# Second attention: the order of a batch's eight projection jobs, with the value job of the batch's own tokens moved from place 5 to place 7

## What is computed

```python
q = (draft_hidden @ Wq.T).reshape(bsz, draft_len, H, HD)          # H = 16 heads, HD = 128
kv_in = jnp.concatenate([context_hidden, draft_hidden], axis=1)   # 128 context + 128 own tokens
k = (kv_in @ Wk.T).reshape(bsz, total_len, KVH, HD)               # KVH = 4
v = (kv_in @ Wv.T).reshape(bsz, total_len, KVH, HD).transpose(0, 2, 1, 3)
q = _rope(_rms_norm(q, q_norm_w), draft_position_ids)
k = _rope(_rms_norm(k, k_norm_w), full_position_ids)
probs = jax.nn.softmax(jnp.einsum('bhqd,bhkd->bhqk', q, k) * SCALE, axis=-1)
attn = jnp.einsum('bhqk,bhkd->bhqd', probs, v)
return attn @ Wo.T
```

## Time and profile before

| what | value |
|---|---|
| median of 3 runs | 3103.31 us (3097.90 to 3106.26) |
| profiled execution | 3106.21 us, span 3104.41 us, mean granted TensorE clock 0.97 |
| busy in the span: PE, DVE, ACT, POOL | 2848.2, 1829.6, 1703.5, 1741.2 us |
| second attention | about 2026 to 2814 us of the span |
| its steady part, 2116 to 2760 us: PE, DVE, ACT, POOL busy | 600.91, 555.51, 441.20, 417.19 of 644 us |

### The profile page before, as it was taken

How to read it: one execution, slowest core, us unless ns; L and a number is a source line. 1 busy time by engine, 2 the same in 40 slices (tenths; PEclk the granted TensorE clock), 3 DMA queues, 4 the chain that set the end, 5 groups by cost and what they waited for, 6 DMA issues and landing times. The chain is left out here.

```text
span 3104.4 us, 57661 instructions
## 1 busy us (share of the span) xinstructions
PE 2848.2 (92%) x16353; PEld 1637.9 (53%) x16354; DVE 1829.6 (59%) x5590; ACT 1703.5 (55%) x4562; POOL 1741.2 (56%) x2443
## 2 busy tenths in 40 slices
PE   4699999999999969999999999769999999985998
PEld 2366666666666635555555554335444444443665
DVE  4366666666666655444344344458888888863443
ACT  5578777877778732333233223346666666661332
POOL 6467777777777534554444455366666666631222
PEclk9799999999999989999999999889999999997999
DMA  6711121112111153554555456535555545657444
GB/s 241 251 42 56 51 86 48 48 55 79 58 48 55 54 200 120 161 157 125 147 159 151 137 141 186 141 80 113 122 113 123 122 112 122 123 106 286 80 83 70
DMA packets 467529, 360.89 MB, mean 116 GB/s; under 512 B 295520, under 2 KB 366304, under 8 KB 467424
## 3 DMA queue, kind: packets, MB, share of 16 engines
q1 hardware_dynamic: 404912, 282.85, 32.1%
q0 software_dynamic: 16496, 37.79, 6.3%
q10 hardware_dynamic: 46016, 38.99, 4.4%
HBM read 186.23 MB, written 110.39 MB: 96 GB/s over the span
## 5 line engine op out<-in xcount | busy, mean ns | idle before, releaser
L1393 POOL TENSOR_TENSOR e_st<-e_st,e_ws_tile 128x1024 f32<-128x1024 f32 x64 | 123.8, 1935 | 428.1 <-PE e_y L1149 417.2
L752 ACT ACTIVATE a_nrm<-a_mm,a_sc_t 128x128 f32<-128x128 f32 x768 | 290.8, 474 | 123.6 <-POOL a_sc_t L905 123.4
L603 DVE BATCH_NORM_STATS2 a_st<-a_mm 128x6 f32<-128x128 f32 x768 | 170.7, 285 | 289.5 <-PE a_mm L440 206.5
L439 PE MATMUL a_mm<-a_w_hi,a_xq_hi 128*128 128x512 f16 x768 | 296.6, 386 | 22.7 <-POOL a_xq_lo L887 15.7
L1187 ACT ACTIVATE e_hh<-e_ha 128x512 f16<-128x512 f32 x128 | 76.3, 596 | 411.7 <-PE e_ha L1134 410.1
L440 PE MATMUL a_mm<-a_w_hi,a_xq_lo 128*128 128x512 f16 x768 | 296.4, 386 | 0.0
L1282 DVE SCALAR_TENSOR_TENSOR e_hl<-e_ha,e_hh 128x512 f16<-128x512 f32 x128 | 88.4, 691 | 351.6 <-ACT e_hh L1187 351.2
L904 POOL TENSOR_TENSOR a_sc_t<-a_sc_t,a_mhalf 128x4 f32<-128x4 f32 x192 | 203.2, 1058 | 119.0 <-DVE a_sc_t L610 118.7
L1147 PE MATMUL e_y<-e_w2h,e_hh 128*128 128x512 f16 x640 | 242.6, 379 | 0.0
L1148 PE MATMUL e_y<-e_w2l,e_hh 128*128 128x512 f16 x640 | 242.6, 379 | 0.0
L1149 PE MATMUL e_y<-e_w2h,e_hl 128*128 128x512 f16 x640 | 242.6, 379 | 0.0
(11 more groups left out here) (366 smaller groups left out, 8246.6 us busy)
## 6 DMA issues: line engine op xcount, KB each, us to landing
e_st<-in_w SPq DMA_DIRECT2D x128, 512.0 KB, 4.2
disp<-a_empty SPq DMA_DIRECT2D x16, 2084.0 KB
e_st<-in_w1b SPq DMA_DIRECT2D x32, 352.0 KB, 3.1
disp<-a_empty SPq DMA_DIRECT2D x4, 2605.0 KB, 22.8
e_xb<-disp SPq DMA_DIRECT2D x40, 260.5 KB, 4.3
e_xb<-disp ACTq DMA_DIRECT2D x40, 260.5 KB
a_cx<-in_ctxT SPq DMA_DIRECT2D x32, 256.0 KB, 3.3
a_stage<-in_wprojT SPq DMA_DIRECT2D x16, 512.0 KB, 4.7
```

The source lines that it names most:

```text
L439: pe.matmul(out, xq_hi[:, n, c, :], w_hi[:, t, c, :], start=(c == 0), stop=False)
L752: ins = act.activation(nrm[:, n % 2, i * P:(i + 1) * P], src[:, i * P:(i + 1) * P], ACT.Identity, bias=sc_t[:, n % 2, 3, i:i + 1], scale=s ...
```

## The change

In the list of jobs, VD moves from place 5 to place 7; Q2 and Q3 move one place forward, to 5 and 6. `NORM1`, `V1`, the waits on banks and all buffers by even and odd follow from the list. No instruction is added or left out.

```diff
-JOBS1 = ["KC", "KD", "Q0", "VC", "Q1", "VD", "Q2", "Q3"]
+JOBS1 = ["KC", "KD", "Q0", "VC", "Q1", "Q2", "Q3", "VD"]
 NJ1 = len(JOBS1)
 NORM1 = [t for t, j in enumerate(JOBS1) if j[0] != "V"]
 V1 = [t for t, j in enumerate(JOBS1) if j[0] == "V"]
```

## The result

The changed kernel takes 3117.18 us (median of 4 runs, 3112.62 to 3119.38) against 3102.64 us (3097.9 to 3106.26) for the kernel before, run beside it: ratio 1.0046, 95% interval 1.0034 to 1.0058. It is slower by about 14.5 us, more than the 0.3% (9.3 us) that the prediction took as the least that can be told from no change. The profiled execution took 3116.52 us (span 3114.7).

The account below looks back on a forecast made before the run. The prediction took a closed ring of engines waiting for each other as the bound, TensorE only following. 14 periods gave +14.0 us, the first batch +1, the last -2: +13 on the 3103.31 median, 3116 us, range 3099 to 3134.

Parts of the forecast that it names:

- the ring: VectorE, GpSimd, ScalarE and SyncE wait for each other from slot 5 to the next slot 5, 46.02 us a batch.
- the ends: First and last batch, outside the 14 periods: +1 us for the first, -2 us for the last.
- GpSimd's queue: Slots 5 and 6: job 5's scales, tables, then job 6's scales put job 6's normalisation 3.0 us later, disturbance included.
- The collisions: GpSimd operations lengthened beside VectorE: +0.4 us on the tables, 0.5 us on job 6's five short operations.
- rival 1: No collision on GpSimd: a period changes by about 0, 3102 us; chance 0.26.
- rival 3: Full exclusion between VectorE and GpSimd: both collisions at their upper end, 1.4 us more a period, 3136 us; chance 0.15.
- Slot 7 to slot 1: VectorE: value's low half adds 0.60 us, job 7's 1.47 us wait goes; slot 1's low probabilities start 1.4 us later.
- TensorE: Job 1 waits for the value's low half; job 2's products reach VectorE at 2447.7, last by 0.4 us.
- Slots 2 to 5: +1.8 us enters; the maximum of slot 3 is 1.5 us later, the next slot 5 1.0 us later.
- The swallowed 0.5: Two small slacks on ScalarE, before slot 3's exponentials and at the normalisation, take up 0.5 us of the delay.
- my +1: The first batch, with the same GpSimd queue, was forecast 1 us longer.
- my 13: Whole kernel: 14 periods give +14.0 us, first batch +1, last batch -2, together +13.

Follow-up runs that it names:

- e1_tabs_early: The changed kernel with GpSimd's table multiplications moved to after slot 3's products; 3078.46 us, ratio 0.9917.
- e8_vd_at_6_banks: The kernel before with VD at place 6, Q3 last, and jobs 6 and 7 using banks 1 and 2; 3084.76 us, ratio 0.9957.
- e9_all_three: e8_vd_at_6_banks with the tables after slot 3's products and the first batch's input scales ahead of its tables; 3082.57 us, ratio 0.9938.
- e3_job1_free: The changed kernel with the product tile of the last value job put in another bank; 3114.55 us, ratio 1.0037.
- e6_vd_at_6: The kernel before with VD at place 6 and Q3 last, banks and tables left as they were; 3125.15 us, ratio 1.0075.
- e7_tabs_plus_four: The changed kernel with four of the six table multiplications done a second time after a wait; 3166.86 us, ratio 1.0207.
- e4_tabs_twice: The changed kernel with all six table multiplications done twice, the second time after a wait; 3174.81 us, ratio 1.0223.

## Why the prediction was right

It said 3116 us for a measured 3117.18, and 47.0 us for a period that is 47.09. The queue on GpSimd and the way of the delay around the ring were right; the ends were not, and that the whole time came out within 1.2 us is in part luck. By its own steps:

- **GpSimd's queue** (the term that decides): job 6's normalisation was put 3.0 us later and is 2.9 (15.80 against 12.90). e1_tabs_early shows that 2.77 us of it are the tables with what they push job 6 into.
- **The collisions** had about the right size, and one had another partner. I had 0.4 for the low half of job 5 on the tables and 0.5 for p_low on the five short operations of job 6. The tables took 2.52 us, no longer than before. VectorE beside them:

```profile
2435.29 0.84 DVE L1731 TENSOR_TENSOR a_nql<-a_nrm,a_nqh 128x512 f16<-128x512 f32 x1 [0.29 <-ACT a_nqh L1889]
2436.05 1.66 DVE L1750 SCALAR_TENSOR_TENSOR a_pql<-a_pr,a_ri,a_pqh 128x256 f16<-128x256 f32 x4
```

The first short operation, 2435.53 to 2436.19, lies beside the low half of job 5 (to 2436.13) and not beside p_low: 0.66 us instead of the 0.21 of job 7's scales in e8_vd_at_6_banks. The other four, beside p_low, took 0.35, 0.27, 0.31 and 0.30 instead of 0.24, 0.20, 0.20 and 0.19, and so 0.40 more. Together +0.85 for the 0.9. So neither rival 1 (nothing) nor rival 3 (2.35) holds. Another short operation shows the same: the one that follows the tables in e8_vd_at_6_banks lies beside the low half of job 5, and in e9_all_three, where the tables are elsewhere, it lies beside none:

```profile
2418.82 0.65 POOL L2010 TENSOR_TENSOR a_rm<-a_rm 128x8 f16<-128x8 f16 x1
```

```profile
2419.20 0.20 POOL L2014 TENSOR_TENSOR a_rm<-a_rm 128x8 f16<-128x8 f16 x1
```

By the rule of the Trainium skill that the prediction named (page "SBUF — State Buffer", section "Who interferes with whom"), each could wait for a whole instruction of VectorE. (The page says "for the whole instruction" of VectorE's two-port modes; of two SBUF inputs it says that they contend, by an exclusive lock.) The rows do not contradict it, but the price is lower than rival 3's. The first operation ends 0.06 us after the low half does. From the second to the sixth operation the starts are 0.43, 0.35, 0.40 and 0.38 us apart, as p_low's four parts start every 0.40 us; without p_low, in e8_vd_at_6_banks, they are 0.27 to 0.32 apart. That would be one operation in each part, each waiting only for what is left of it, which loses some 0.1 and not 0.42. This reading is mine and no run tests it.
- **Slot 7 to slot 1**: maximum of slot 1 forecast at 22.6 us, found at 22.43; the wait of 1.47 for the normalised values is gone.
- **TensorE** last by 0.4 before the statistics of job 2: 0.38. e3_job1_free shows that this margin, and not the wait of 1.0 at job 1, is the most that this step is worth.
- **Slots 2 to 5**: the statistics of job 2 come 1.69 us later in the frame (forecast 1.8), the maximum of slot 3 1.71 (1.5), the next slot 5 1.24 in this batch and 1.02 in the mean (1.0). The swallowed 0.5 of the prediction was 0.47.
- **The ends** were mis-sized in the same direction. Counted from GpSimd's first operation of the stage (L1949, at 2021.70; 2022.28 before), slot 5 of batch 1 comes at 72.34 us against 72.42: for my +1 there is -0.1. The maximum of slot 3 still comes 2.1 us later there (58.76 against 56.62), and the step from it to slot 5 takes it back (13.58 against 15.80). The granted clock is 1.00 in that step and was 0.89 in the kernel before; no run tells whether this is the cause or goes with another. From slot 5 of batch 15 to the start of the last scatter I had -2, and found -3.4 (64.5 against 67.9).
- **The sum.** The 14 periods give 14.3 for my 14.0, and with the ends the stage is 14.3 - 0.1 - 3.4 = 10.9 us longer (rounded from the rows) for my 13. The stage began 0.6 us earlier in the profiled execution, so the profiled pair differs by 10.3 us, and the medians by 14.5. My 13 lies between the two. The start of the stage alone varies by 6.4 us over the eleven profiled executions, though nothing ahead of it was changed (2018.69 to 2025.08).

Open: where the 4 us lie by which pair and medians differ, since the other executions have no trace.

## What to carry to other kernels

Before moving jobs in an order that several in-order engines share, look on every engine for work that is tied to a place and not to a job: here six small multiplications, free after a value job, cost 2.8 us a batch between two query jobs, and moved to an idle place they turned a loss of 0.5% into a gain of 0.8%. A wait is worth at most the margin by which it ends last, not its length. And after a gain, look for the next thing in the queue before counting a second one.

## What the runs showed of the hardware

TensorE's granted clock fell to the lower of its two levels after idle times of a few us in an otherwise busy loop, and not always at the same idle time.

- In the kernel before and the changed one, whose longest waits of TensorE in the steady stretch are 1.9 and 1.7 us, the clock stays at 1.00.
- In e6_vd_at_6 the wait is 2.40 us in each of the middle batches. In every second one the products after it slow down (0.43 us apart), the clock is 0.96 and the period 1.7 us longer; in the others it is 1.00, as in the first period with its wait of 2.75 us.
- In e7_tabs_plus_four the wait is 3.7 us (4.15 in the first period). The clock is 0.93 in the first period and from the sixth to the thirteenth, 0.97 in the second, fourth and fifth, and 1.00 in the third.
- In e4_tabs_twice, with 4.43 us (4.85 in the first), it is 0.93 in every period.

So the length of the idle time does not decide alone, and what else does was not tested. The price: with the clock falling, a delay of 2.16 us on GpSimd made a period 3.9 us longer (e7_tabs_plus_four, later batches), and 1.9 to 2.3 us where it held.

Six small GpSimd multiplications (128x128) took 2.51 us in the kernel before and 3.70 beside low halves on VectorE (e1_tabs_early); an operation of 0.20 us took 0.65 beside one low half (e8_vd_at_6_banks).
